# Routed feed-forward tiles of 128 slots with an expert each, gating and scatters moved between attention steps, and a last stage whose blocks overlap

## What is computed

```python
def _L0_ffn_ref(x, gate_w, expert_bias, w_up, w_down):       # 8 experts, top 2, I = 512
    logits = jnp.einsum('bsh,eh->bse', x, gate_w) + expert_bias
    weights = jax.nn.softmax(logits, axis=-1)
    top_w, top_i = jax.lax.top_k(weights, K)
    top_w = top_w / (jnp.sum(top_w, axis=-1, keepdims=True) + GATE_EPS)
    ...
    for e in range(E):
        h = jax.nn.gelu(jnp.einsum('bsh,ih->bsi', x, w_up[e]), approximate=False)
        y = jnp.einsum('bsi,hi->bsh', h, w_down[e])
        out = out + sparse_w[..., e:e + 1] * y
    ...                                                      # layer norm of out
    return out + x
x = x + 0.5 * _L0_ffn_ref(_layernorm(x, axis=-1), ...)
x = x + _L0_attn_ref(_layernorm(x, axis=-1), ...)            # causal linear attention, 16 heads of 64, cos/sin weights
x = x + 0.5 * _L0_ffn_ref(_layernorm(x, axis=-1), ...)
```

## Time and profile before

| | |
|---|---|
| time, median of 3 runs | 1254.38 us (1247.94 to 1255.65) |
| profiled execution, its own time | 1255.69 us |
| its span in the trace | 1253.9 us |
| granted TensorE clock, mean over the span | 0.919 |
| instructions | 32419 |
| busy: PE / weight loads / DVE / ACT / POOL | 73% / 59% / 79% / 57% / 63% |
| setup, layer norm, first routing | 0 to 114 us |
| first feed-forward (46 pairs) | 114 to 281 us |
| attention (64 steps) | 281 to 1046 us |
| second feed-forward (39 pairs) | 1046 to 1205 us |
| last stage | 1205 to 1254 us |

### The profile page before, as it was taken

One profiled execution on the slowest core, in us unless ns is written; L12 is line 12 of the kernel. 1 busy time (PEld: TensorE's weight loads), 2 busy tenths in 40 slices (PEclk: granted clock), 3 DMA queues, 4 the chain that ended last, 5 costly groups with the idle time before them and its releaser, 6 DMA issues.

```text
span 1253.9 us, 32419 instructions
## 1 busy us (share of the span) xinstructions
PE 917.1 (73%) x12594; PEld 745.9 (59%) x12594; DVE 985.5 (79%) x2130; ACT 711.1 (57%) x1033; POOL 790.1 (63%) x671
## 2 busy tenths in 40 slices
PE   3303989778977897887888887696887786779900
PEld 2302979666755675665666665575665575679900
DVE  7887787887769899889899888887688975857722
ACT  2112767557754675665666685474665564657712
POOL 2188735817865676776765664498884675577754
PEclk9999999999997998998998998898898887889955
DMA  9332424329990000000000000000000001223251
GB/s 337 131 109 73 141 84 118 92 76 185 196 188 9 8 9 8 6 9 8 6 8 2 2 2 2 1 15 22 23 15 2 6 17 49 62 80 96 78 165 59
DMA packets 99074, 78.26 MB, mean 62 GB/s; under 512 B 8080, under 2 KB 89360, under 8 KB 98672
## 3 DMA queue, kind: packets, MB, share of 16 engines
q1 hardware_dynamic: 89568, 58.18, 19.8%
q0 software_dynamic: 8640, 17.78, 4.6%
q10 hardware_dynamic: 720, 0.23, 0.1%
HBM read 30.07 MB, written 46.09 MB: 61 GB/s over the span
## 4 chain that ended last, share of the span: by engine, by line
DVE 26%; POOL 25%; PE 23%; issue 14%; ACT 7%; DMA 3%; DVEq 0%; POOLq 0%; SPq 0%; ACTq 0%
POOL arena_a L1824 5%; DVE arena_b L1716 5%; POOL xs L782 4%; POOL xs L814 3%; DVE arena_a L1674 3%; PE bank L1477 3%; POOL arena_a L1806 3%; ACT arena_c L1589 3%; DVE arena_c L1712 2%; POOL arena_b L843 2%; PE bank L1401 2%; POOL arena_c L1828 2%; DVE xn_new L477 2%; PE bank L1403 2%; PE bank L1402 2%
## 5 line engine op out<-in xcount | busy, mean ns | idle before, releaser
L1824 POOL TENSOR_TENSOR arena_a<-arena_a 128x1024 f16<-128x1024 f32 x64 | 139.1, 2173 | 70.3 <-ACT arena_a L1589 69.8
L1589 ACT ACTIVATE arena_c<-arena_a 128x1024 f16<-128x1024 f32 x64 | 67.6, 1057 | 176.4 <-DVE arena_a L1674 176.4
L1806 POOL TENSOR_TENSOR arena_a<-arena_b,trig_rows 128x512 f32<-128x512 f32 x128 | 160.0, 1270 | 6.8 <-issue 6.8
L1699 DVE TENSOR_TENSOR arena_b<-bank,decay 128x512 f32<-128x512 f32 x128 | 82.5, 686 | 53.4 <-PE bank L1477 52.8
L1589 ACT ACTIVATE arena_b<-arena_b 128x512 f16<-128x512 f32 x128 | 78.3, 629 | 66.1 <-DVE arena_b L1699 66.1
L1401 PE MATMUL bank<-wo_hi,arena_c 128*128 128x128 f16 x256 | 53.8, 240 | 75.2 <-DVE arena_c L1683 75.2
L1321 POOL DMA_INDIRECT ys<-arena_b,row_at x78 | 84.8, 1087 | 36.3 <-issue 22.6
L814 POOL DMA_INDIRECT xs<-xhl,slot_idx x64 | 78.5, 1227 | 40.4 <-issue 40.4
L995 ACT ACTIVATE arena_c<-bank,s_pre 128x1024 f32<-128x1024 f32 x46 | 51.2, 1113 | 92.2 <-PE bank L930 86.5
L1827 POOL TENSOR_TENSOR arena_c<-arena_c 128x130 f16<-128x130 f32 x64 | 30.6, 479 | 114.6 <-ACT arena_c L1639 114.5
L1716 DVE TENSOR_TENSOR arena_b<-arena_b 128x1024 f16<-128x1024 f32 x64 | 101.2, 1581 | 0.0
(11 more groups left out here) (320 smaller groups left out, 4275.4 us busy)
## 6 DMA issues: line engine op xcount, KB each, us to landing
xs<-blank SPq DMA_DIRECT2D x8, 2210.0 KB, 32.4
xs<-arena_c SPq DMA_DIRECT2D x2, 3072.0 KB, 18.5
arena_b<-xs SPq DMA_DIRECT2D x46, 128.0 KB
ys<-arena_b SPq DMA_DIRECT2D x46, 128.0 KB, 1.8
arena_b<-xs SPq DMA_DIRECT2D x39, 130.0 KB, 2.3
arena_a<-in_w_up SPq DMA_DIRECT2D x1, 2048.0 KB, 12.6
arena_b<-in_w_down SPq DMA_DIRECT2D x1, 2048.0 KB, 13.6
arena_a<-ys SPq DMA_DIRECT2D x8, 256.0 KB, 4.4
```

Source lines behind the costliest of these rows:

```text
L1589: nc.scalar.activation(dst, src, ACT.Copy, scale=scale).then_inc(done, 1)
L1699: i = nc.vector.tensor_tensor(probs[:, h * BLK:(h + 1) * BLK].rearrange("p (c i) -> p c i", c=TPB), ps_so[:, h, :].rearrange("p (c i) -> p ...
L1806: i = nc.gpsimd.tensor_tensor(q_trig[h], q_relu[h], trig_rows[:, bass.ds(u * BLK, BLK)], ALU.mult)
L1824: nc.gpsimd.tensor_tensor(q_lo, arena_a[:, 0:2 * BLK], q_hi, ALU.subtract).then_inc(a["q_lo_done"], 1)
```

## The change

**Tiles of 128 slots.** Each expert's rows are padded to a multiple of 128 slots, and the two tiles of a pair have an expert each. NPAIR goes from 23 to 20 (46 to 40 pairs in the first feed-forward) and SECOND from 39 to 36; FULL counts tiles now, 40, which is 20 pairs. The table of tiles has 40 entries instead of 24, and there are 5 packed words instead of 3. `up` has for each of two tiles 4 chunks of 3 matmuls with 128 columns; `down` runs over the tiles and then over the chunks; both work out the weight addresses for each tile. SP's `load` in the second feed-forward reads a row number and issues a DMA for each tile.

**Attention.** The gating is cut in three pieces, (0,), (1 to 4), (5 to 9), with `route_next` in the fourth step, from (4,6) and from (6,6) on. `route_product` stands in (5,0) and (7,0) and is waited for in (5,1) and (7,1). The scatters start at (5,2) and (7,2), with one tile in most steps and two in (5,3), (5,6), (7,3) and (7,5).

**The last stage.** The two choices of a token lie beside each other in DRAM (`place`), so a block is one DMA. The small arrays have a place for every tile; DVE adds the choices of block b+1 ahead of the statistics of block b and no longer waits for ACT; mean, variance and power are taken for groups of blocks, TAIL.

The diff, cut to its core:

```diff
-SLOTS, NPAIR, NTABLE = 24 * 2 * P, 23, 24
+SLOTS, NPAIR, NTABLE = 40 * P, 20, 40
-FULL = -(-(2 * P * 24 - E * (2 * P - 1)) // (2 * P))
-SECOND = NTOK * TOPK // (2 * P) + E - 1
+FULL = 2 * (-(-(2 * P * 24 - E * (P - 1)) // P) // 2)
+SECOND = -(-(NTOK * TOPK // P + E - 1) // 2)
+NPACK = NTABLE // 8
...
             def expert_at(packs, p):
-                at = ((packs[p // 8] >> (3 * (p % 8))) & 7) * I
-                return nc.s_assert_within(at, 0, (E - 1) * I, skip_runtime_bounds_check_because="three bits")
+                ats = [((packs[t // 8] >> (3 * (t % 8))) & 7) * I for t in (2 * p, 2 * p + 1)]
+                return [nc.s_assert_within(at, 0, (E - 1) * I, skip_runtime_bounds_check_because="three bits") for at in ats]
...
-                for c in range(CH):
-                    w_hi, w_lo = (w[:, bass.ds(at_e + c * P, P)] for w in (wup_hi, wup_lo))
-                    dst = ps_pre[G % 2][:, c // 2, (c % 2) * 2 * P:(c % 2 + 1) * 2 * P]
-                    nc.tensor.matmul(dst, w_hi, x_hi, start=True, stop=False)
-                    nc.tensor.matmul(dst, w_hi, x_lo, start=False, stop=False)
-                    i = nc.tensor.matmul(dst, w_lo, x_hi, start=False, stop=True)
+                for s in range(2):
+                    x = tuple(part[:, s * P:(s + 1) * P] for part in (x_hi, x_lo))
+                    for c in range(CH):
+                        w_hi, w_lo = (w[:, bass.ds(at[s] + c * P, P)] for w in (wup_hi, wup_lo))
+                        cols = (c % 2) * 2 * P + s * P
+                        dst = ps_pre[G % 2][:, c // 2, cols:cols + P]
+                        nc.tensor.matmul(dst, w_hi, x[0], start=True, stop=False)
+                        nc.tensor.matmul(dst, w_hi, x[1], start=False, stop=False)
+                        i = nc.tensor.matmul(dst, w_lo, x[0], start=False, stop=True)
...
-                for c in range(CH):
-                    w_hi, w_lo = (w[:, bass.ds(at_e + c * D, D)] for w in (flat_dn_hi, flat_dn_lo))
-                    for s in range(2):
+                for s in range(2):
+                    for c in range(CH):
+                        w_hi, w_lo = (w[:, bass.ds(at[s] + c * D, D)] for w in (flat_dn_hi, flat_dn_lo))
...
-                packs = [pe.value_load(tile_e[0:1, i % 2, g:g + 1], min_val=0, max_val=2 ** 24 - 1) for g in range(3)]
+                packs = [pe.value_load(tile_e[0:1, i % 2, g:g + 1], min_val=0, max_val=2 ** 24 - 1) for g in range(NPACK)]
...
-            for b in range(NBLK):
-                v.wait_ge(in_yl[b], 32)
-                nc.vector.tensor_tensor(yl[b][:, 0, :, :], yl[b][:, 0, :, :], yl[b][:, 1, :, :], ALU.add
...
-                if b:
-                    v.wait_ge(last_z, b)
...
+            both_choices(0)
+            for group, (b0, b1) in enumerate(TAIL):
+                for b in range(b0, b1):
+                    if b + 1 < NBLK:
+                        both_choices(b + 1)
+                    v.wait_ge(last_sum, b + 1)
...
+                for s in range(2):
+                    t = (2 * p + s) % FULL
+                    row = sp.value_load(tile_row[0:1, int(part), t:t + 1], min_val=0, max_val=NROWS - 2 * P)
+                    sp.dma_start(xs_in2[p % NXS][:, s, :], d["xs2"][bass.ds(row, P), :]).then_inc(in_xs2[p % NXS], 16)
...
-                if n == 5 and hp == 3:
+                if n == 5 and hp == 0:
                     route_product(pe, 2)
-                if n == 7 and hp == 1:
+                if n == 7 and hp == 0:
                     route_product(pe, 3)
...
+                for i, first in ((2, 4), (3, 6)):
+                    at = NHP * (n - first) + hp - 6
+                    if 0 <= at < 3:
+                        for j in ((0,), (1, 2, 3, 4), (5, 6, 7, 8, 9))[at]:
+                            gating(v, i, j)
+                    if at == 3:
+                        route_next(v, i - 2)
...
-                        at = NHP * (n - 5) + hp - 5
-                        if 0 <= at < 11:
-                            scatter_next(g, 0, ((0,), (1,), (2,), (3, 4), (5, 6), (7, 8), (9, 10), (11, 12), (13,), (14,),
-                                                (15,))[at])
+                        at = NHP * (n - 5) + hp - 2
+                        if 0 <= at < 14:
+                            scatter_next(g, 0, ((0,), (1, 2), (3,), (4,), (5, 6), (7,), (8,), (9,), (10,), (11,), (12,), (13,),
+                                                (14,), (15,))[at])
```

More of the change, by code:

```diff
@@ L1204, in load_packs @@
                 pe.wait_ge(tiles_done, part + 1)
[L1205 removed]
+                packs.append([pe.value_load(tile_e2[0:1, part, g:g + 1], min_val=0, max_val=2 ** 24 - 1) for g in range(NPACK)])
             load_packs(0)
@@ L1342, in second_pool @@
                 scatter_y(p)
-            for b in range(NBLK):
-                power(b)
-                if b:
-                    add(b - 1)
-            add(NBLK - 1)
+            for group in range(len(TAIL)):
+                power(group)
+                if group:
+                    add(group - 1)
+            add(len(TAIL) - 1)
         BEFORE_LAST = 4
@@ L1353, in load @@
             def load(p):
-                part, t = (0, p) if p < FULL else (1, p - FULL)
-                if t == 0:
+                part = 2 * p >= FULL
+                if 2 * p in (0, FULL):
                     sp.wait_ge(tiles_done, part + 1)
-                    if part == 0:
+                    if not part:
                         sp.wait_ge(scat2[0], 16 * 2 * GROUPS[0][1])
@@ L1375, in second_sync @@
             for b in range(NBLK):
-                for choice in range(2):
-                    rows = d["ys2"][choice * NTOK + b * BLK:choice * NTOK + (b + 1) * BLK, :]
-                    sp.dma_start(yl[b][:, choice, :, :], rows.rearrange("(t p) f -> p t f", p=P)).then_inc(in_yl[b], 16)
+                rows = d["ys2"][b * 2 * BLK:(b + 1) * 2 * BLK, :]
+                sp.dma_start(yl[b].rearrange("p t c f -> p (t c f)"), rows.rearrange("(p r) f -> p (r f)", p=P)
+                             ).then_inc(in_yl[b], 16)
             out = d["out"].rearrange("(t p) d -> p t d", p=P)
```

152 lines of the change are left out of this document (76 added, 76 removed).

## The result

The changed kernel takes 1299.26 us (median of 4 runs, 1292.38 to 1303.09) where the kernel before takes 1254.53: a ratio of 1.0363, with a 95% interval of 1.0320 to 1.0407. It is slower by some 45 us; the forecast was 1283, in a range of 1258 to 1305. The profiled execution was the fastest of the four, with a span of 1290.4 us, 36.5 more than the span before; the other 8 us of the 45 lie in runs without a trace. The three runs without one were granted a higher mean clock (0.936 against 0.905), so a lower clock isn't what makes them longer.

A forecast was written before the change was run, and what follows sets the result against it. PE's queue of register instructions was taken to set the feed-forwards' pace at 4.4 us a pair. 27.4 - 11 + 23 - 11.5 = +28 us on a span of 1253.9 gave 1282, or 1283 us at the median, range 1258 to 1305.

The forecast's parts named there:

- PE's queue: Both feed-forwards: register instructions and waits, 39 x 0.1125 us, make 4.4 us a pair (4.1 to 4.6) and set the pace.
- Array: Both feed-forwards: 52 matmuls of 128 columns at 0.0557 us take 2.90 us a pair, so the change costs nothing there.
- Loads of packed words: PE's queue at the half boundary and pair 20: five words take 3.2 us, and the queue hides nothing of it.
- The start: Up to the first gelu: 0.4 us later, for wider tables in two routing steps.
- The end of the first feed-forward: Last gelu to stage end: 12.0 us becomes about 13 to 14, as two last `down` take 1.9 instead of 1.3.
- The end of the second feed-forward: Last gelu to SP's first read: 10 us, since POOL keeps up with slower pairs and no longer ends last.
- Attention: Attention steps: -11 us together, from -8 for two-tile steps, 5 gained on gating, and some 2 lost to wider tables.
- The last stage: From first sum to last addition: 35.7 us becomes 24.2, so -11.5, as DVE no longer waits for ACT.
- That the queue hides: Rival, feed-forwards: the array bounds at 2.90 us a pair, 1204 us, chance 6 in 100; another 6 for a partial case.
- The clock: Rival, feed-forwards: PE's clock drops more often to 1.2 GHz, giving 1300 to 1330 us; chance 8 in 100.
- that rival: Rival, attention: steps with gating shrink to the others' length, -42 us in place of -11, 1252 us; chance 8 in 100.

The follow-up runs named there:

- the run with shared addresses: Changed kernel with both tiles of a pair using the first one's expert, one address serving six matmuls, 18 register instructions a pair: 1219.69 us, ratio 0.9745.
- the run with doubled addresses: Kernel before, tiles and pairs unchanged, but each tile works out its own weight addresses, 36 register instructions a pair: 1346.52 us, ratio 1.0716.

## Why the prediction was right, and where its sizes were off

**PE's queue.** Right in its mechanism, and it carried the forecast. The spacing was too small: 0.119 us instead of 0.1125, so 4.65 us a pair instead of 4.4; the upper bound of 4.6 was a hair too low. The reading was lost in rounding: the rows give the ends of the 16 intervals to a tenth, 1111.8 and 1113.6, and the trace has them at 1111.755 and 1113.645, which is 1.89 us, or 0.118 for each. Over 74 intervals 0.25 us is 18.5, and 1283 + 18.5 is 1301.5, beside 1299 measured; but that this fits so well is luck. In the traces the two feed-forwards, from gelu to gelu, are only 5.4 and 2.5 us longer than forecast, since the sum took every interval at the full pace and added a wait on top. The first gelus, the one behind the half boundary, and the first and the seventh of the second feed-forward (ACT's timeline):

```profile
116.81 1.11 ACT L1001 ACTIVATE arena_c<-bank,s_pre 128x1024 f32<-128x1024 f32 x1 [48.58 <-PE bank L936]
119.01 1.09 ACT L1001 ACTIVATE arena_c<-bank,s_pre 128x1024 f32<-128x1024 f32 x1
121.25 1.11 ACT L1001 ACTIVATE arena_c<-bank,s_pre 128x1024 f32<-128x1024 f32 x1
125.99 1.11 ACT L1001 ACTIVATE arena_c<-bank,s_pre 128x1024 f32<-128x1024 f32 x1 [2.44 <-PE bank L936]
...
208.85 1.11 ACT L1001 ACTIVATE arena_c<-bank,s_pre 128x1024 f32<-128x1024 f32 x1 [6.17 <-PE bank L936]
...
1074.43 1.11 ACT L1242 ACTIVATE arena_c<-bank,s_pre 128x1024 f32<-128x1024 f32 x1 [8.52 <-PE bank L1192]
...
1101.78 1.11 ACT L1242 ACTIVATE arena_c<-bank,s_pre 128x1024 f32<-128x1024 f32 x1 [6.24 <-PE bank L1192]
```

The first two intervals take 2.2 us each, as PE has no `down` to do yet: 4.9 us less than two full ones. In the second feed-forward the first six, which hold the wait for the last gating, take 27.4 us together, no more than six of 4.65: the 6 us that were set down for that wait on top of the full pace did not come. By the traces the forecast of +27.9 is 8.6 short of the 36.5 measured; 7.9 of that lie in these two stretches, and the other terms' errors nearly cancel. What lies between the traces and the median, another 8 us, no run explains.

The rule of the Trainium skill that was weighed there ("Perfetto Trace Analysis", the section on the per-engine timelines, on instructions of the sequencer) agrees with the rows: those of the register instructions are 32 to 46 ns long, and they cost 119 each. What that page of the Trainium skill has pushed behind the execution is a semaphore update, not a next stage.

**Array.** Right: 2.90 us for 52 matmuls of 128 columns, as the run with shared addresses shows, weight loads and all. By the Trainium skill's figure of about 81 ns ("TensorE: Matmul & The Clock Gate", the section on the back-to-back issue gap) that would be an estimated 4.2 us; the trace has 56 ns, and it decides.

**Loads of packed words.** Three words were priced at 2.0 us, five at 3.2. The interval at the half boundary is 8.46 us, 3.8 above the median of 4.65, and the one at pair 20 of the second feed-forward 8.40. The queue hides none of it, as forecast; the size was slightly small.

**The start.** +0.4 was forecast, and the two traces differ by -2.1. The three other traces with the new tiles have their first gelu at 119.6 us, 0.7 later than before, so the -2.1 does not come with the tiles.

**The end of the first feed-forward.** +2 was forecast, for two slower `down`, and +5.2 measured. That was the wrong reason: the run with doubled addresses has the slower `down` too, with 46 pairs, and takes 15.7 us there, less than the kernel before. What moves the stretch is DVE's work that is left behind the last of fewer pairs.

**The end of the second feed-forward.** POOL's lag was to go away; it did, by 7.5 us of the 10 forecast. From 1245.12 on, the last five scatters still follow each other 1.26 us apart.

**Attention.** The sum, -11, lies near the -14.5 of the traces, but for reasons that were not the prediction's. It gave 8 us to the steps with two tiles and 5 to the gating. The schedule alone is worth 5 us (1.5 to 9), and 7 of the 14.5 lie in steps that the change does not touch. The step that failed is taking the difference of two groups of steps for the price of a tile or of a part of the gating. The five steps with two tiles hold one stall of DVE behind POOL, 5.8 us long. The three steps under gating, 15.3 us each, stand for ten with gating or `route_next` that take 10.1 to 19.5, 13.8 on average; the eight of the changed kernel still take 14.4 on average. Its steps with one tile take 9.1 to 13.1 us.

**The last stage.** -11.5 forecast, -10.5 in the traces, -13 (7 to 19) by the run with it alone. Right in size, and DVE's part is: it no longer waits for ACT and is done 17.5 us after its first sum, where 18.4 was forecast. But POOL ends last, from the timelines of POOL and DVE:

```profile
1267.42 2.02 POOL L1347 TENSOR_TENSOR first_rstdh<-first_var,minus_half 128x8 f32<-128x8 f32 x1 [0.27 <-DVE first_var L1331]
...
1273.55 0.16 DVE L1331 TENSOR_SCALAR first_var<-first_mv 128x4 f32<-128x4 f32 x1
...
1277.91 3.70 POOL L1357 TENSOR_TENSOR x_tok<-x_tok,arena_c 128x512 f32<-128x512 f32 x3
```

From 1267.42 on POOL works without another wait, and three additions are still to do when the last power is through. So 7.9 us lie between DVE's end and the last addition's, where the sum had 5.8.

**The rivals.** That the queue hides was ruled out by the trace and by the runs with 28 and 36 register instructions. The clock did not fall: 0.99 and 0.97. Attention did not give back the 42 us of that rival: the schedule alone gives 5.

## What to carry to other kernels

Where matmuls take their weights from an address in a register, count the register instructions and waits on PE's queue per unit of work and price each by the distance between starts (0.119 us here), not by its row; compare that with the array's time before cutting matmuls shorter or giving each its own address. The smaller padding saved six pairs of 46, and paid for it with 18 more register instructions in each of the rest. When steps differ in length, look for one line whose maximum stands far above its median before pricing the work that happens to lie in the long steps, and compare a stretch that the change does not touch, to see how far two traces differ by themselves.

## What the runs showed of the hardware that I had not expected

DVE's subtraction of two operands in SBUF stands still while POOL runs tensor operations back to back: 7.44 us instead of 1.2, through five POOL operations, until they end and, 0.16 us later, a scatter begins. Elsewhere a gap of 0.02 us was enough: in the changed kernel POOL's split ends at 602.19, its next operation starts at 602.21, and the subtraction ends at 603.29, 1.1 us behind the split. What decides which of the two engines goes on is not shown: in the rows of the long one the subtraction starts 0.6 us ahead of POOL's split, while a scatter runs on POOL (996.93 to 997.89), and is held even so. The Trainium skill, page "SBUF — State Buffer", section "SBUF: two separate sides", says that a DVE instruction with two SBUF inputs and a POOL instruction that reads SBUF exclude each other for a whole instruction, and that the loser fully blocks. The traces agree that it blocks; but the hold lasted over five instructions and not one. A wait on POOL's queue that makes the gap brought the longest down to 3.82 us and the time down by 0.45% (0.1 to 0.8).
